# One PSUM bank for the row scores and three for the small jobs in a fused two-layer attention and expert kernel

## The chip, the core and the metric

The kernel runs on one core of one Trainium2 chip. The metric is the device time of one launch in microseconds (us). Every time below comes from this kernel's timed runs or from one profiled execution of it.

The engines are named as the profile names them. PE is TensorE (matrix multiplications; PEld is its weight load), DVE is VectorE, ACT is ScalarE, POOL is GpSimd, and SP is SyncE, which here only issues DMAs. PE writes its results into PSUM, which has eight banks of 128 partitions by 512 fp32 numbers. In this kernel DVE and ACT read them out, and POOL works only on SBUF.

## What is computed

The input is `x` with 8 batches of 256 rows and 128 features, and a context of the same shape. Four stages are added to `x` one after the other: a 16-head attention of the context, a mixture of 32 experts, a second attention, and a top-1 mixture of 8 experts. The change lies in the second attention:

```
xn, ln = layernorm(ctx), layernorm(layernorm(x))
q = ln @ Wq                                   # 16 heads of 64
k, v = [xn; ln] @ Wkv                         # 512 keys per batch
sim = (rmsnorm(q) * g_q * scale) @ (rmsnorm(k) * g_k).T
x  = x + softmax(sim) @ v @ Wout + bout
```

## The kernel before, in words

`attend_layer1` (from L1223) is the second attention. A **batch** is one of the 8. A **unit** is half of a batch's heads (8 of 16), so there are 16 units. A **step** is one pair of heads, so a unit has 4 steps and the stage has 64. Batches 1 to 6 run in a hardware loop over `b` (`flow`, L1297); the first and the last batch are written out apart.

Each step has the same parts, and each part is a word in the table `ORDER` (L1090), one string for each of the four steps of a unit:

- `rXY` (L1457, L1733): PE computes the scores of head X for 128 queries Y against all 512 keys, once and coarsely, and DVE takes their maximum into `neg_max`. This is done two steps ahead of its use. There are four in a step.
- `m` (L1448, L1627): PE transposes the four maxima of the next step, ACT copies them to `neg_rows`, and SP places them by a DMA as one more row of `q_high`.
- `sXY` (L1560, L1561, L1676 to L1681): PE computes the exact scores of head X for half Y of the keys; ACT takes the exponential twice, once rounded to fp16 and once in fp32. There are four in a step.
- `LXY` (L1738) and `P1` (L1385): the low part of the exponentials, for head 0 by DVE and for head 1 by POOL.
- `w0`, `w1` (L1473 to L1475): PE weighs the values with the probabilities of the step before; `n` (L1761, L1764): DVE divides by the sums; `a` (L1483, L1632): PE transposes the result and ACT copies it.
- `o`, `do` (L1492, L1771): once per batch, the output projection of the batch before, in fp32, and its addition to `x` by DVE.
- For the unit that follows: `k`, `q`, `v` (L1413 to L1415) are the projections of one tile of 128 rows. For `k` and `q` ACT copies the result and squares it (L1595, L1597), and `dk`, `dq` (L1703) is DVE's sum of squares. For `v` ACT copies it and `dv` (L1727) is DVE's low part. `root` (L1705 to L1721) is DVE's reciprocal square root of all the sums, 12 short instructions. `norm` (L1368, L1372) is POOL's scaling by it, `hi` (L1607) is ACT's rounding, and `low` (L1380) is POOL's low part. `tk`, `tq` (L1442, L1751) is PE's transposition of a normed tile and DVE's copy of it; SP then copies a part of it to `k_high` or `q_high` by a DMA.

Every engine walks through the same four strings and does its own share of each word, in the order of the words. So the order on each queue, and how far one engine can run ahead of another, are both set by this table. `plan_step` leaves out the words that a first or last batch does not have.

The eight PSUM banks of the stage are shared out at L1263 to L1267: `RBANKS` (2) for the row scores, `SBANKS` (3) for the exact scores, one for the weighing, and `MBANKS` (2) named `misc`. The words of `MISC` (L1137: `k q v tk tq o m a`) take the misc banks in turn, and `number` (L1168) gives each its bank and its count. PE may write a misc bank again when its last user has been read out (`emptied`, L1417). With two banks that is the word before the last one. For the row scores, PE waits at L1455 until the maximum before the last has been taken:

```
pe.wait_ge(max_done, n - RBANKS + 1)
pe.matmul(row_scores[qt % RBANKS][:], ...)
```

At the third string's first `r00`, PE also waits for the DMAs of all six transposed tiles of the next unit (L1538). At each step's first `s00` it waits for the DMA that `m` started (L1545).

Before the loop, `unit_start` (L1141) writes out the preparation of the first unit, and ends with eight row products (two steps' worth), `m`, and `root`.

Of the kernel before, what the change touches and what calls it, by code (L numbers as in the profile page):

```python
# [949 lines left out]
def prepare_layer1(nc, io, keep):  # L950
# [124 lines left out]

KQ = [("k", t) for t in range(KT)] + [("q", t) for t in range(QT)]
ROWS_AHEAD = 2
MBANKS = 2
WIDE = 2
SBANKS = 3  # L1080
RBANKS = 2


LOWS = ("V", "P")
# [3 lines left out]
ATTENDED_BY = "A"  # L1088
HALVES = 2 * PU * 2 * (KT // WIDE)
ORDER = [  # L1090
# [4 lines left out]
]  # L1095
NEWTON = 3
RSQRT_BITS = float(0x5f3759df)
# [70 lines left out]
def number(events, bank, counts):  # L1168


    counts, out, uses = list(counts), [], {}
    for event in events:
        use = uses[event[1]] if event[0] == "d" else (bank, counts[bank])
        out.append((event, use))
        if event[0] in MISC:
            uses[event] = use
            counts[bank] = counts[bank] + 1
            bank = (bank + 1) % MBANKS
    return out, bank, counts


def steps_of(first, last):
    return [plan_step(s, first, last) for s in range(2 * PU)]


def totals(events):
    return number(events, 0, (0,) * MBANKS)[2]


START_EVENTS = number(START, 0, (0,) * MBANKS)[0]  # L1190


class Batch:
# [3 lines left out]
    def __init__(self, b, first=False, last=False):  # L1197
# [4 lines left out]
        else:  # L1202
            one, whole = totals(sum(steps_of(True, False), [])), totals(sum(steps_of(False, False), []))
            self.counts = [start[i] + one[i] - whole[i] + whole[i] * b for i in range(MBANKS)]

# [17 lines left out]
def attend_layer1(nc, io, keep):  # L1223
# [3 lines left out]
    with ExitStack() as ctx:  # L1227
# [3 lines left out]
        def psum(name, shape):  # L1231
            return ctx.enter_context(nc.psum_tensor("e_" + name, shape, F32))

        def sem(name):
            return ctx.enter_context(nc.semaphore("e_" + name))
# [26 lines left out]

        row_scores = [psum(f"row_scores{i}", [P, NK1]) for i in range(RBANKS)]  # L1263

        scores = [psum(f"scores{i}", [P, WIDE, S]) for i in range(SBANKS)]
        mix = psum("mix", [P, 2, S])
        misc = [psum(f"misc{i}", [P, 512]) for i in range(MBANKS)]  # L1267
        mixed = mix[:, :, 0:QT * (D1 + 1)].rearrange("p i (t c) -> p i t c", t=QT)

        cleared, fixed = sem("cleared"), sem("fixed")  # L1270
        misc_ready, misc_taken = [sem(f"misc_ready{i}") for i in range(MBANKS)], [sem(f"misc_taken{i}") for i in range(MBANKS)]
        summed_sq, inv_steps, inv_done, normed, hi_done, low_done, v_high = (sem(n) for n in (
# [138 lines left out]
        def _(pe):  # L1411
# [38 lines left out]
            def rows(q, par, p, i, qt):  # L1450

                n = 4 * q + 2 * i + qt
                if not (isinstance(n, int) and n < RBANKS):

                    pe.wait_ge(max_done, n - RBANKS + 1)  # L1455
                h = 2 * p + i
                pe.matmul(row_scores[qt % RBANKS][:], q_high[par][0:MASK1 + 1, h, P * qt:P * qt + P], k_high[par][0:MASK1 + 1, h, :],  # L1457
                          start=True, stop=True).then_inc(rows_ready, 1)
# [232 lines left out]
        def _(dve):  # L1691
# [38 lines left out]
            def maximum(q, buf, i, qt):  # L1730
                n = 4 * q + 2 * i + qt
                dve.wait_ge(rows_ready, n + 1)
                dve.tensor_reduce(neg_max[buf][:, 2 * i + qt:2 * i + qt + 1], row_scores[qt % RBANKS][:], AX.X, ALU.max, negate=True).then_inc(max_done, 1)  # L1733

# [647 lines left out]
```

## Time and profile before

| what | us |
|---|---|
| timed runs, median of 3 (lowest, highest) | 1325.49 (1323.56, 1330.16) |
| the profiled execution's own time | 1331.85 |
| its span, first to last instruction | 1330.1 |
| the second attention, from its first projection to its last addition to `x` | about 534 to 1158 |
| DVE, PE, ACT, POOL busy over the span | 959.7, 952.3, 771.7, 591.5 |

The span and the time differ by 1.75 us, which lies around the first and the last instruction. In a timeline row the first number is the start of a group of equal instructions in us from the span's start, the second how long it lasted, and what stands in brackets at the end is the idle time of that engine before it and who ended it. Two neighbouring instructions of one engine overlap a little in the records, so the time that an instruction takes away from its engine is the distance from its start to the next start.

### The profile page before, as it was taken

To read this page: it belongs to the slowest core of one execution; us is meant where nothing else is said; L and a number is where in the kernel's file an instruction comes from. 1 tells how busy PE (TensorE), PEld (TensorE's weight loads), DVE (VectorE), ACT (ScalarE), POOL (GpSimd) and SP (SyncE) were. 2 spreads that over 40 slices of the span, in tenths; PEclk is the share of its full clock that TensorE was granted. 3 is DMA by queue.
4 is the path that set the end of the run, shared out by engine and by line. 5 is a ranking of instruction groups with operands and counts; after the bars stand their busy time and mean duration, and the time that the engine had idled before them with its cause. 6 is when DMAs were issued, how large, how long until landed. Compare 5 with 4: busy or idle time off the path is not lost. (4 is left out here: it accounts for less than half of the span.)

```text
span 1330.1 us, 28004 instructions
## 1 busy us (share of the span) xinstructions
PE 952.3 (72%) x9389; PEld 621.0 (47%) x9394; DVE 959.7 (72%) x1847; ACT 771.7 (58%) x1404; POOL 591.5 (44%) x505
## 2 busy tenths in 40 slices
PE   0378888742999921558887988888788888637655
PEld 0235555521444420125665666666565666514344
DVE  8568989767666668448888787878787887358930
ACT  1227777730555522529988897978787897441022
POOL 8010000021777730537767576767666674220324
PEclk9779999965999965759999999999899999859978
DMA  4311100010000020011111111111111111140140
GB/s 197 87 15 19 22 14 12 1 38 0 24 24 19 11 99 0 1 28 25 27 21 27 25 25 27 25 26 22 22 18 27 19 27 22 51 167 1 38 126 24
DMA packets 73839, 46.72 MB, mean 35 GB/s; under 512 B 55056, under 2 KB 70911, under 8 KB 72646
## 3 DMA queue, kind: packets, MB, share of 16 engines
q1 hardware_dynamic: 72296, 42.40, 13.3%
q0 software_dynamic: 1440, 2.82, 0.6%
q8 instruction: 80, 1.31, 0.4%
q14 instruction: 23, 0.19, 0.0%
HBM read 26.52 MB, written 8.77 MB: 27 GB/s over the span
## 5 line engine op out<-in xcount | busy, mean ns | idle before, releaser
L1385 POOL TENSOR_TENSOR e_p_lo<-e_probs,e_p_hi 128x1024 f16<-128x1024 f32 x64 | 136.3, 2129 | 127.2 <-ACT e_probs L1678 127.2
L1733 DVE TENSOR_REDUCE e_neg_max<-e_row_scores 128x1 f32<-128x512 f32 x256 | 170.1, 683 | 21.3 <-PE e_row_scores L1457 20.8
L1676 ACT ACTIVATE e_p_hi<-e_scores 128x512 f16<-128x512 f32 x256 | 153.1, 598 | 53.0 <-PE e_scores L1561 50.8
L1560 PE MATMUL e_scores<-e_q_stack,e_k_stack 128*128 128x256 f16 x512 | 127.2, 278 | 5.8 <-DVE e_p_lo L1738 5.4
L1368 POOL TENSOR_TENSOR e_raw<-e_raw,e_inv 128x512 f32<-128x512 f32 x96 | 98.9, 1043 | 70.4 <-DVE e_inv L1718 70.4
L1561 PE MATMUL e_scores<-e_q_high,e_k_high 128*128 128x256 f16 x512 | 127.3, 278 | 0.0
L1380 POOL TENSOR_TENSOR e_natural<-e_raw,e_natural 128x512 f16<-128x512 f32 x96 | 109.2, 1157 | 28.2 <-ACT e_natural L1607 27.5
L1457 PE MATMUL e_row_scores<-e_k_high,e_q_high 65*128 65x512 f16 x256 | 96.2, 395 | 33.7 <-DVE e_neg_max L1733 21.8
L716 POOL TENSOR_TENSOR c_h_lo<-c_hidden,c_h_hi 128x512 f16<-128x512 f32 x68 | 78.9, 1160 | 78.0 <-ACT c_h_hi L835 75.8
L1473 PE MATMUL e_mix<-e_v_cols,e_p_hi 128*128 128x65 f16 x1024 | 109.5, 194 | 4.4 <-POOL e_p_lo L1385 3.3
L1474 PE MATMUL e_mix<-e_v_cols,e_p_hi 128*128 128x64 f16 x1024 | 109.6, 196 | 0.0
L1475 PE MATMUL e_mix<-e_v_cols,e_p_lo 128*128 128x65 f16 x1024 | 109.1, 193 | 0.0
L1473 PEld LDWEIGHTS e_mix<-e_v_cols,e_p_hi 128*128 128x128 f16 x1024 | 96.6, 97 | 12.1 <-POOL e_p_lo L1385 4.1
L1474 PEld LDWEIGHTS e_mix<-e_v_cols,e_p_hi 128*128 128x128 f16 x1024 | 96.4, 98 | 7.9
L844 ACT ACTIVATE c_gated<-c_gate_ps 128x512 f32<-128x512 f32 x68 | 40.6, 597 | 100.3 <-PE c_gate_ps L742 100.3
L1738 DVE TENSOR_TENSOR e_p_lo<-e_scores,e_p_hi 128x512 f16<-128x512 f32 x128 | 87.6, 684 | 14.0 <-ACT e_scores L1681 12.3
L1475 PEld LDWEIGHTS e_mix<-e_v_cols,e_p_lo 128*128 128x128 f16 x1024 | 96.5, 100 | 0.0
L535 DVE TENSOR_REDUCE b_neg_max<-b_row_scores 128x2 f32<-128x512 f32 x128 | 83.2, 685 | 16.8 <-PE b_row_scores L374 15.2
L543 DVE TENSOR_TENSOR b_p_lo<-b_probs,b_p_hi 128x1024 f16<-128x1024 f32 x64 | 78.0, 1219 | 20.9 <-ACT b_p_hi L508 12.0
L505 ACT ACTIVATE b_probs<-b_scores 128x1024 f32<-128x1024 f32 x64 | 65.9, 1030 | 46.1 <-PE b_scores L394 45.4
L1442 PE MATMUL e_misc<-ident,e_natural 128*128 128x128 f16 x768 | 63.9, 232 | 37.8 <-ACT e_neg_rows L1627 18.2
L1703 DVE TENSOR_REDUCE e_sum_sq<-e_squares 128x8 f32<-128x512 f32 x96 | 65.1, 679 | 24.7 <-ACT e_squares L1597 19.7
(367 smaller groups left out, 2877.1 us busy)
## 6 DMA issues: line engine op xcount, KB each, us to landing
e_k_high<-e_k_stack SPq DMA_DIRECT2D x64, 128.0 KB, 2.7
e_q_high<-e_q_stack SPq DMA_DIRECT2D x32, 128.0 KB, 2.6
w<-in_w SPq DMA_DIRECT2D x2, 2048.0 KB, 10.1
c_w<-in_w SPq DMA_DIRECT2D x17, 192.0 KB, 2.4
placed_scratch<-in_no_rows SPq DMA_DIRECT2D x1, 2313.0 KB, 18.2
a_mask_q<-in_mask_q SPq DMA_DIRECT2D x1, 2048.0 KB, 10.2
a_mask_k<-in_mask_k SPq DMA_DIRECT2D x1, 2048.0 KB, 14.6
parts_scratch<-a_parts SPq DMA_DIRECT2D x2, 1024.0 KB, 4.0
```

Of the source, the lines that this page charges most:

```text
L1368: nc.gpsimd.tensor_tensor(raw[par][:, j], raw[par][:, j], bc(inv[:, HU * j:HU * j + HU], (P, HU, D1), 2), ALU.mult).then_inc(normed, 1)
L1380: nc.gpsimd.tensor_tensor(natural[:, j, :, at], raw[par][:, j], natural[:, j, :, hi], ALU.subtract).then_inc(low_done, 1)
L1385: nc.gpsimd.tensor_tensor(p_lo[buf][i][:], probs[i][:], p_hi[buf][i][:], ALU.subtract).then_inc(lo_done[i], 1)
L1457: pe.matmul(row_scores[qt % RBANKS][:], q_high[par][0:MASK1 + 1, h, P * qt:P * qt + P], k_high[par][0:MASK1 + 1, h, :], start=True, stop=T ...
L1473: pe.matmul(out, p_hi[buf][i][:, kt, at], values[:, 0:D1 + 1], start=first, stop=False, skip_group_check=True)
L1474: pe.matmul(out[:, 0:D1], p_hi[buf][i][:, kt, at], values[:, D1 + 1:2 * D1 + 1], start=False, stop=False, skip_group_check=True)
L1475: mm = pe.matmul(out, p_lo[buf][i][:, kt, at], values[:, 0:D1 + 1], start=False, stop=last, skip_group_check=True)
L1560: pe.matmul(out, k_stack[hf][:, h, cols], q_stack[hf][:, h, :], start=(kt % 2 == 0), stop=False, skip_group_check=True)
L1561: mm = pe.matmul(out, k_high[hf][:, h, cols], q_high[hf][:, h, :], start=False, stop=True, skip_group_check=True)
L1676: act.activation(p_hi[p % 2][i][:, at, :], scores[n % SBANKS][:], ACT.Exp).then_inc(exp_done, 1)
L1733: dve.tensor_reduce(neg_max[buf][:, 2 * i + qt:2 * i + qt + 1], row_scores[qt % RBANKS][:], AX.X, ALU.max, negate=True).then_inc(max_done, 1)
L1738: dve.tensor_tensor(p_lo[buf][i][:, at, :], scores[n % SBANKS][:], p_hi[buf][i][:, at, :], ALU.subtract).then_inc(lo_done[i], 1)
```

## The change

The constants and the table are all that is changed. The row scores get one bank instead of two, the misc words three instead of two; the total stays at eight. The words of each string are the same, in another order.

```
-MBANKS = 2
+MBANKS = 3
 WIDE = 2
 SBANKS = 3
-RBANKS = 2
+RBANKS = 1
...
 ORDER = [
-    "r00 s00 P1 norm2 w0 s01 tk0 a hi2 L00 r01 m norm3 tk1 hi3 s10 s11 low2 r10 k0 r11 L01 dk0 k1 w1 low3 n dk1",
-    "r00 norm4 hi4 P1 s00 m s01 s10 tk2 tk3 r01 norm5 L00 r10 hi5 w0 k2 L01 w1 tq0 s11 n a r11 tq1 low4 low5 dk2",
-    "L00 s00 k3 s01 o do w0 m P1 dk3 L01 s10 w1 n q0 r00 s11 r01 dq0 q1 r10 v0 r11 dq1 dv0 root a",
-    "L00 P1 w0 r00 norm0 s00 m s01 v1 dv1 s10 hi0 a r01 norm1 hi1 w1 r10 low0 s11 v2 low1 n v3 L01 dv2 dv3 r11",
+    "norm2 s00 s01 norm3 r00 hi2 m hi3 tk0 w0 P1 L00 k0 r01 dk0 s10 k1 r10 L01 w1 tk1 low2 s11 low3 r11 a dk1 n",
+    "k2 s00 m tk2 norm4 r00 norm5 hi4 s01 L00 tk3 hi5 s10 r01 a L01 w0 r10 w1 P1 n tq0 s11 tq1 low4 r11 dk2 low5",
+    "s00 o k3 a s01 P1 w0 q0 L00 s10 do r00 L01 w1 n v0 r01 dk3 m dv0 s11 r10 dq0 q1 dq1 r11 root",
+    "P1 a v1 v2 r00 norm0 m norm1 L00 w0 s00 s01 r01 dv2 hi0 hi1 s10 low0 s11 dv1 L01 w1 low1 r10 v3 n r11 dv3",
 ]
```

The wait of a row product becomes `max_done >= n`: each one waits until the maximum just before it has been taken. A misc word waits for the third before it. The bank numbers of all engines, the counts of the semaphores and `Batch`'s totals are worked out from the same two constants.

## Rows read from the trace of the kernel before

**Rows 1.** Waits on PE, 670 to 1035 us (five batches): who waited, total us, times, longest.

```profile
PE e_row_scores L1457 <- DVE e_neg_max L1733: 17.5, 13, 3.5
PE e_misc L1442 <- ACT e_neg_rows L1627: 11.6, 10, 1.3
...
PE e_misc L1483 <- ACT e_squares L1597: 7.3, 10, 0.9
```

**Rows 2.** Timeline of POOL, one unit: first `norm`, last two `low`, next unit's first `norm`.

```profile
762.17 2.04 POOL L1368 TENSOR_TENSOR e_raw<-e_raw,e_inv 128x512 f32<-128x512 f32 x2 [3.00 <-DVE e_inv L1718]
...
779.72 2.29 POOL L1380 TENSOR_TENSOR e_natural<-e_raw,e_natural 128x512 f16<-128x512 f32 x2
...
795.09 2.04 POOL L1368 TENSOR_TENSOR e_raw<-e_raw,e_inv 128x512 f32<-128x512 f32 x2 [3.02 <-DVE e_inv L1718]
```

**Rows 3.** Timeline of PE: `a`, `r11`, `tq1`, then the third string up to `r00`.

```profile
781.84 0.38 PE L1483 MATMUL e_misc<-ident,e_attended 128*128 128x128 f32 x2
782.06 0.38 PE L1457 MATMUL e_row_scores<-e_k_high,e_q_high 65*128 65x512 f16 x1
782.43 0.62 PE L1442 MATMUL e_misc<-ident,e_natural 128*128 128x128 f16 x8
782.89 0.27 PE L1560 MATMUL e_scores<-e_q_stack,e_k_stack 128*128 128x256 f16 x1
...
783.45 0.39 PE L1413 MATMUL e_misc<-wkv_hi,lat_hi 128*128 128x512 f16 x1
...
784.11 0.27 PE L1560 MATMUL e_scores<-e_q_stack,e_k_stack 128*128 128x256 f16 x1
...
784.54 0.19 PE L1473 MATMUL e_mix<-e_v_cols,e_p_hi 128*128 128x65 f16 x1
...
785.28 0.27 PE L1448 MATMUL e_misc<-ident,e_neg_max 128*4 128x128 f32 x1
...
787.21 0.38 PE L1457 MATMUL e_row_scores<-e_k_high,e_q_high 65*128 65x512 f16 x1
787.43 0.27 PE L1560 MATMUL e_scores<-e_q_stack,e_k_stack 128*128 128x256 f16 x1
```

**Rows 4.** Timeline of DVE, same unit: `n`, a maximum, `r00` with `r01`.

```profile
782.22 0.17 DVE L1761 RECIPROCAL e_inverse<-e_mix 128x4 f32<-128x4 f32 x1
...
782.76 0.68 DVE L1733 TENSOR_REDUCE e_neg_max<-e_row_scores 128x1 f32<-128x512 f32 x1
783.36 0.68 DVE L1751 COPY e_q_stack<-e_misc 128x512 f32<-128x512 f32 x1
...
788.02 1.28 DVE L1733 TENSOR_REDUCE e_neg_max<-e_row_scores 128x1 f32<-128x512 f32 x2
```

**Rows 5.** A row product that waited for its bank, on DVE and then on PE.

```profile
762.63 0.68 DVE L1733 TENSOR_REDUCE e_neg_max<-e_row_scores 128x1 f32<-128x512 f32 x1
...
763.37 0.39 PE L1457 MATMUL e_row_scores<-e_k_high,e_q_high 65*128 65x512 f16 x1 [0.69 <-DVE e_neg_max L1733]
```

**Rows 6.** ACT, same unit: first exponential of an `s`, then the next word.

```profile
783.52 0.60 ACT L1676 ACTIVATE e_p_hi<-e_scores 128x512 f16<-128x512 f32 x1
...
784.64 0.59 ACT L1595 COPY e_raw<-e_misc 128x512 f32<-128x512 f32 x1
```

**Rows 7.** DMA issues, 534 to 1160 us: name, count, KB each, median us to landing.

```profile
e_q_high<-e_q_stack SPq DMA_DIRECT2D x32, 128.0 KB, 2.6
```

**Rows 8.** The output projection on PE, and DVE's next maxima after it.

```profile
748.38 3.74 PE L1492 MATMUL e_misc<-wout,nrm 128*128 128x128 f32 x32
...
755.04 1.35 DVE L1733 TENSOR_REDUCE e_neg_max<-e_row_scores 128x1 f32<-128x512 f32 x2 [0.23 <-PE e_row_scores L1457]
```

**Rows 9.** Start of the stage: row products on PE, maxima and `root` on DVE.

```profile
578.29 1.03 PE L1457 MATMUL e_row_scores<-e_k_high,e_q_high 65*128 65x512 f16 x2 [4.23 <-DMA e_q_high<-e_q_stack]
...
578.94 2.68 DVE L1733 TENSOR_REDUCE e_neg_max<-e_row_scores 128x1 f32<-128x512 f32 x4 [4.14 <-PE e_row_scores L1457]
...
585.21 0.18 DVE L1712 TENSOR_SCALAR e_sum_sq<-e_sum_sq 128x48 f32<-128x48 f32 x1
```

**Rows 10.** PE at the loop's end: the next pass's first instruction.

```profile
802.38 0.39 PE L1457 MATMUL e_row_scores<-e_k_high,e_q_high 65*128 65x512 f16 x1 [3.75 <-issue]
```

## The prediction, made before the changed kernel was run

> **What bounds the kernel now.** I read the busy time by stage first (in the second attention no engine is full, and PE, DVE and ACT are about equally busy), then who waits for whom, then the timelines of one unit on every engine. Only those show what closes the circle.
>
> POOL gives it away. At each unit it stands idle for 3.0 us, until DVE's `root` is done, and then works without a gap until the last `low` ends at 779.72 + 2.29 = 782.01; the next unit's first `norm` starts at 795.09 [rows 2]. So the period of a unit is 795.09 - 762.17 = 32.92 us, in two legs. **Leg A**, from `root` to `tq1`: 782.43 - 762.17 = 20.26 us of POOL's work, after which PE turns the last tile [rows 2, 3]. **Leg B**, from `tq1` back to the next end of `root`: 795.09 - 782.43 = 12.66 us. PE walks from `tq1` to `r00`, 787.21 - 782.43 = 4.78 us, in which it hardly waits [rows 3]; DVE takes the first maximum 0.81 us later, at 788.02, since it is still behind, and then runs through seven words and `root` without a pause until 795.09 [rows 4, 2].
>
> PE's waits for misc banks (11.6 and 7.3 us in five batches) and for row banks (17.5 us) [rows 1] lie mostly in leg A. POOL hides them there, so long as `tq1` itself is not late.
>
> **Slots.** What a word takes from its engine, start to start. PE [rows 3]: `a` 782.06 - 781.84 = 0.22; `tq` 0.46; `k` or `q` 784.11 - 783.45 = 0.66; `s` 784.54 - 784.11 = 0.43; `w` 785.28 - 784.54 = 0.74; `r` 787.43 - 787.21 = 0.22. DVE [rows 4]: 0.60 for a maximum or any other word of 512 columns, `n` 782.76 - 782.22 = 0.54. `root` is 795.09 - 788.02 - 7 x 0.60 = 2.87, its hand-over to POOL in it. An `s` takes ACT 784.64 - 783.52 = 1.12 [rows 6].
>
> **The change, leg A.** POOL's words between `root` and `low5` are the same ones in both tables, `P1` of strings one and two among them; only their order differs. The new table puts `P1` of the second string behind `norm5`. So PE's `w1` and ACT's exponential of `s10` wait for it there (POOL needs about 4.5 us for `norm4` and `norm5` first), but both are done before `low5`. I laid out the new words with the slots above, and ACT delivers every `hi` before POOL asks for it, the closest (`hi2`) by half a microsecond. I take 0 for leg A. Bounds: below 0 nothing, since POOL is already without a gap; above, half a microsecond a unit if a `hi` comes late.
>
> **Leg B, PE's part.** From `tq1` to `r00` the new table has `tq1 r11 s00 k3 a s01 w0 q0 s10`: 0.46 + 0.22 + 0.43 + 0.66 + 0.22 + 0.43 + 0.74 + 0.66 + 0.43 = 4.25 us, against 4.78. `m` and `w1` have gone behind `r00`. The gain is 0.5 us. It is safe from the DMAs, though barely: DVE has copied `tq1` about 1.1 us after PE started it (my estimate: 0.46 for PE, 0.60 for DVE), I allow 0.3 us to the issue, and with 2.6 us to landing [rows 7] that is 4.0 us.
>
> **Leg B, DVE's part.** DVE's words before `r00` are now only `r11`, `dk2` and `L00`. It runs dry for about 1.5 us and starts `r00` 0.42 us after PE does (a product of 0.38 us [rows 3] and a hand-over). Then come `r00 L01 n r01 dk3 dv0 r10 dq0 dq1 r11 root`: 9 x 0.60 + 0.54 + 2.87 = 8.81 us, against 7.07. Three words, `L01`, `n` and `dk3`, that the old table had before `r00` now stand behind it: 1.74 us. I add 0.15 us for `dq1`, which waits for ACT. The new leg B is 4.25 + 0.42 + 8.81 + 0.15 = 13.63 us against 12.66: **+1.0 us a unit**. Bounds: 0, if DVE's dry time gets filled after all, and +1.8, if PE's half microsecond is not gained.
>
> **Units with an output projection.** `o` blocks PE for 3.7 us [rows 8]. Before, DVE's `r00` came at 755.04, and PE had started `o` at 748.38. Between `o` and `r00` the new PE order has `k3 a s01 w0 q0 s10` = 0.66 + 0.22 + 0.43 + 0.74 + 0.66 + 0.43 = 3.14 us, and before `o` one `s` and one `k` fewer but `r11` more (-0.87). So DVE's `r00` comes at 748.38 - 0.87 + 3.6 + 3.14 + 0.42 = 754.67, 0.4 us earlier, and its tail is 1.8 us longer: +1.4 us.
>
> **One row bank.** A product now waits for the maximum just before. The hand-shake is 0.42 us from product to maximum and 763.37 - 762.63 = 0.74 us from there to the next product [rows 5], 1.16 us in all. In the new table there is another word of DVE's between any two maxima, so that the two take at least 1.14 to 1.2 us anyway. Its price is zero wherever PE arrives in time. **Three misc banks** take PE's waits in leg A away, which POOL hides: zero too. If `tq1` were late for any reason, both would count at once (rivals).
>
> **Where the queues stand otherwise.** SP issues the same DMAs; `m`'s go later in the third string, but its `s00` is also later by then, 4 us or more behind. PE's 3.75 us at the loop's end [rows 10] has nothing to do with the table. The new step behind it brings `hi2` about 1.2 us sooner, but the step before it ends about that much later (its `r11` and `v3` wait for DVE): zero.
>
> **Start of the stage.** Eight products follow each other with nothing between them. At the lower clock there, the old ones took 585.21 - 578.29 = 6.92 us to `root` [rows 9]. With one bank each takes 0.65 (578.94 - 578.29) + 0.74 = 1.39 us, with `m` 11.2 us: +4.3. Three misc banks let the first transposes start earlier, which I put at -0.9. Together +3.4 us, bounds 0 and +4.3.
>
> **Sum.** Fourteen units are followed by another `root`; six of them have an `o`. 8 x 1.0 + 6 x 1.4 = 16.4, and 3.4 for the start: **+19.8 us**. The profiled execution took 1331.85 us, 6.36 above the median of the runs; against itself the sum gives 1351.7, and on the median's footing 1325.49 + 19.8 = 1345.3. Bounds of the known terms: 14 x 0 + 0 = 0, and 14 x 2.2 + 4.3 = +35.
>
> **Rivals.**
> - *The misc banks pay* (faster). If leg A is paced by PE and ACT rather than POOL, the waits for misc banks go: (11.6 + 7.3) / 5 = 3.8 us a batch [rows 1], over seven batches 26.5, less 3.4 at the start: 1302 us; with half of it, 1316. It decides at `tq1`: if PE gets there more than 0.3 us after `low5` ends in the kernel before, it is right. There it came 0.42 us after, with `r11` just before it, which leaves it a little room. For it also speaks that leg B may hold less of the tail than I think. Chance 0.22.
> - *The one row bank bites everywhere* (slower still). If PE meets an untaken maximum once a step, at the 0.69 us of the one seen [rows 5], 64 steps cost 44 us in place of the 16: about 1373 us. Against it: words stand between all maxima. Chance 0.12.
> - *Nothing moves*: DVE's dry time before `r00` is cover, so that the three moved words cost only what PE's lead gives back; with the start, 1325 to 1332 us. Chance 0.13.
> - *The change does not do what it says.* Banks, waits and counts all come from the two constants, and the sum stays at eight. Chance 0.01.
>
> PE's row product and DVE's maximum took turns over two banks without a wait in most places, and where the bank was missing the wait was 0.69 us [rows 5]. The Trainium skill (Perfetto Trace Analysis, section Optimizing Tensor Performance, Matmuls) says that independent matmul groups should rotate through different PSUM banks, so that reading one out overlaps the next. By that rule the row scores lose what the misc words gain, four products a step against at most eight misc words a step, and the sum would be that of the second rival for the one and of the first for the other; it does not say which is on the path.
>
> **How the numbers follow.** My forecast is 1345 us with a chance of 0.52. The range 1310 to 1360 takes it with nearly all its bounds, the third rival, and the nearer half of the first; it leaves out the second and the full first. A measurement of this kernel can tell about 0.5% (6.6 us) from no change. Faster by more: the first rival and a little of my own low end, 0.24. Within: 0.15. Slower: 0.61.
>
> **What would show it.** Right: POOL still works without a gap from `norm0` to `low5` in about 20 us; its idle time before the first `norm` grows from 3.0 to about 4 us; DVE is idle 1 to 2 us before the third string's `r00`; the period of a unit without `o` or loop end is near 33.9 us; PE's waits for ACT's squares and neg_rows are gone. Wrong: a period of 32 us or less, or a gap in POOL's work inside leg A, which would mean that a `hi` or `P1` has become late.

## The result, and the profile after

The changed kernel is **slower by 1.2%**: 1343.89 us (median of 4 runs, 1339.19 to 1345.48) against 1327.83 us (4 runs, 1323.56 to 1331.29) of the kernel before, a ratio of 1.0117 with a 95% interval of 1.0073 to 1.016. The forecast was 1345.0 us.

The profiled execution took 1342.71 us (span 1340.9). From the first POOL instruction of the second attention to the start of its last addition to `x` it is 1173.26 - 533.87 = 639.39 us, against 1157.54 - 534.43 = 623.11: +16.3, as the medians have it (+16.1). The two profiled executions differ by 10.9 only: what lies behind the stage took 172.5 us in the one of before and 167.7 in the one of after, and holds nothing of the change.

A **plain** unit is one without an `o`.

| from `norm0` to the next unit's `norm0`, us | before | after |
|---|---|---|
| plain unit, the steady ones | 32.90 to 32.93 | 33.16 to 33.27 |
| sum over the 14 units (8 plain, 6 with `o`) | 499.67 | 509.64 |
| of these the 8 plain ones / the 6 with `o` | 263.52 / 236.15 | 266.73 / 242.91 |
| stage start to the first unit's second `norm0` | 53.66 | 56.26 |
| last `norm0` to the last `do` | 69.78 | 73.49 |

So +9.97 in the units, +2.60 at the start, +3.71 at the end: +16.3.

The plain units ran at a granted clock of 1.00 (2.4 GHz) in both kernels, except the first, 33.02 us at 0.84 before and 34.29 at 0.78 after. The units with an `o` did not, and the table shows that this matters (the clock is TensorE's, as a mean over the unit):

| units with `o`, in order | 1 | 2 | 3 | 4 | 5 | 6 |
|---|---|---|---|---|---|---|
| longer by, us | 0.51 | 2.75 | 2.14 | 0.25 | -0.11 | 1.19 |
| clock before | 1.00 | 1.00 | 0.96 | 0.96 | 0.92 | 0.96 |
| clock after | 1.00 | 0.92 | 0.92 | 0.96 | 0.92 | 0.92 |

All but the first hold a turn of the hardware loop, at which PE stands for 3.3 to 3.9 us. Around it the granted clock is at 0.50 (1.2 GHz) for some 4 us, or for some 7, or (once, before) not at all. The unit is over 1 us longer just where the clock is lower than before. So of the 6.8 us of these six units about 3 us (6 x 0.5, by the first) belong to the change itself, an estimate. Whether the new table makes the low stretches longer, or chance does, no run separates: both lengths occur in both kernels.

PE's waits in the changed kernel, 670 to 1050 us (five batches; who waited for whom, total us, times, longest), against [rows 1]:

```profile
PE e_row_scores L1457 <- DVE e_neg_max L1733: 31.2, 51, 1.2
...
PE e_misc L1413 <- DVE e_v_cols L1727: 2.1, 10, 0.2
```

Two things are not in [rows 1] and change how it reads. In the kernel before, `m` waited for a misc bank too, and three of the 13 waits for DVE's maxima are turns of the loop, 3.5 us each, that the profile puts down to DVE:

```profile
PE e_misc L1448 <- DVE e_k_stack L1751: 4.8, 8, 0.8
```

```profile
730.34 0.39 PE L1457 MATMUL e_row_scores<-e_k_high,e_q_high 65*128 65x512 f16 x1 [3.54 <-DVE e_neg_max L1733]
```

So the waits for misc banks fell from 11.6 + 7.3 + 4.8 = 23.7 us to 2.1, and those for row banks grew from about 7 us, in 10 waits, to 31.2 in 51. Read alone, this table says that 22 us were exchanged for 24. The plain unit shows what is left of that. POOL's timeline of one, against [rows 2]:

```profile
769.31 2.04 POOL L1368 TENSOR_TENSOR e_raw<-e_raw,e_inv 128x512 f32<-128x512 f32 x2 [3.27 <-DVE e_inv L1718]
...
786.65 2.27 POOL L1380 TENSOR_TENSOR e_natural<-e_raw,e_natural 128x512 f16<-128x512 f32 x2
790.12 2.13 POOL L1385 TENSOR_TENSOR e_p_lo<-e_probs,e_p_hi 128x1024 f16<-128x1024 f32 x1 [1.20 <-ACT e_probs L1678]
797.47 2.13 POOL L1385 TENSOR_TENSOR e_p_lo<-e_probs,e_p_hi 128x1024 f16<-128x1024 f32 x1 [5.22 <-ACT e_probs L1678]
802.48 2.04 POOL L1368 TENSOR_TENSOR e_raw<-e_raw,e_inv 128x512 f32<-128x512 f32 x2 [2.88 <-DVE e_inv L1718]
```

And PE's, against [rows 3]: `tq0`, then `tq1` with nothing but `s11` ahead of it, and `r00`.

```profile
787.86 0.62 PE L1442 MATMUL e_misc<-ident,e_natural 128*128 128x128 f16 x8 [0.21 <-POOL e_natural L1380]
...
788.98 0.62 PE L1442 MATMUL e_misc<-ident,e_natural 128*128 128x128 f16 x8
...
793.22 0.38 PE L1457 MATMUL e_row_scores<-e_k_high,e_q_high 65*128 65x512 f16 x1
```

POOL works without a gap until 786.65 + 2.27 = 788.92, and `tq1` starts at 788.98. Leg A is 788.98 - 769.31 = 19.67 us, leg B 802.48 - 788.98 = 13.50. Before they were 20.26 and 12.66. Of the 0.59 us that leg A lost, 0.36 are at its end, where `tq1` started 0.42 us behind POOL's last `low` and now starts 0.06 behind it. The other 0.23 are in POOL's own part, 19.84 us before and 19.61 after, mostly a short wait of the kernel before, behind its `norm0` and `norm1`:

```profile
764.39 2.27 POOL L1380 TENSOR_TENSOR e_natural<-e_raw,e_natural 128x512 f16<-128x512 f32 x2 [0.18 <-ACT e_natural L1607]
```

DVE's timeline of the same unit, against [rows 4], from its `L00` to the start of `root`:

```profile
791.54 0.69 DVE L1738 TENSOR_TENSOR e_p_lo<-e_scores,e_p_hi 128x512 f16<-128x512 f32 x1
793.63 0.69 DVE L1733 TENSOR_REDUCE e_neg_max<-e_row_scores 128x1 f32<-128x512 f32 x1 [1.40 <-PE e_row_scores L1457]
...
797.77 1.30 DVE L1703 TENSOR_REDUCE e_sum_sq<-e_squares 128x8 f32<-128x512 f32 x2
799.00 0.68 DVE L1733 TENSOR_REDUCE e_neg_max<-e_row_scores 128x1 f32<-128x512 f32 x1
799.59 0.18 DVE L1712 TENSOR_SCALAR e_sum_sq<-e_sum_sq 128x48 f32<-128x48 f32 x1
```

DVE runs dry for 1.40 us, takes `r00` 0.41 us after PE starts it, and then needs 802.48 - 793.63 = 8.85 us until POOL can start behind `root`. Hold on to one more pair of numbers, which I passed over at first: POOL's `P1` ends at 797.47 + 2.13 = 799.60, and `root` begins at 799.59.

At the start of the stage each row product waits for the maximum before it. PE's timeline and the start of DVE's `root`, against [rows 9]:

```profile
575.96 0.61 PE L1457 MATMUL e_row_scores<-e_k_high,e_q_high 65*128 65x512 f16 x1 [4.56 <-DMA e_q_high<-e_q_stack]
577.35 0.61 PE L1457 MATMUL e_row_scores<-e_k_high,e_q_high 65*128 65x512 f16 x1 [0.79 <-DVE e_neg_max L1733]
...
587.25 0.18 DVE L1712 TENSOR_SCALAR e_sum_sq<-e_sum_sq 128x48 f32<-128x48 f32 x1
```

Product to product it is 1.39 us, the number of the prediction, and from the first product to `root` 587.25 - 575.96 = 11.29 us (forecast 11.2, before 6.92).

### The profile page after: what moved, and what is told of

The parts are those of the page before. It is cut to its first block and busy times, and to the rows that moved or that the text cites. A ratio compares the mean times of both kernels' runs of the same rounds, so it can differ in the third digit from the quotient of the medians.

```text
span 1340.9 us, 27886 instructions
## 1 busy us (share of the span) xinstructions
PE 964.1 (72%) x9394; PEld 626.7 (47%) x9394; DVE 957.7 (71%) x1847; ACT 770.0 (57%) x1404; POOL 594.0 (44%) x505
## 5 line engine op out<-in xcount | busy, mean ns | idle before, releaser
L1733 DVE TENSOR_REDUCE e_neg_max<-e_row_scores 128x1 f32<-128x512 f32 x256 | 175.1, 684 | 72.5 <-PE e_row_scores L1457 72.1
L1457 PE MATMUL e_row_scores<-e_k_high,e_q_high 65*128 65x512 f16 x256 | 102.9, 402 | 56.5 <-DVE e_neg_max L1733 51.4
L1738 DVE TENSOR_TENSOR e_p_lo<-e_scores,e_p_hi 128x512 f16<-128x512 f32 x128 | 87.4, 683 | 11.3 <-ACT e_scores L1681 10.9
L543 DVE TENSOR_TENSOR b_p_lo<-b_probs,b_p_hi 128x1024 f16<-128x1024 f32 x64 | 78.0, 1219 | 20.9 <-ACT b_p_hi L508 11.9
L1703 DVE TENSOR_REDUCE e_sum_sq<-e_squares 128x8 f32<-128x512 f32 x96 | 64.5, 680 | 25.8 <-ACT e_squares L1597 20.9
L877 DVE TENSOR_TENSOR c_upped<-c_up_ps,c_gated 128x512 f32<-128x512 f32 x68 | 47.0, 692 | 49.5 <-PE c_up_ps L742 48.3
```

What stands on the lines that cost most here:

```text
L1738: dve.tensor_tensor(p_lo[buf][i][:, at, :], scores[n % SBANKS][:], p_hi[buf][i][:, at, :], ALU.subtract).then_inc(lo_done[i], 1)
```

## The experiments

All times are medians. A ratio is to the kernel before on the same chip, with its 95% interval. The "circle" below is the dependence of one unit on the last: `root`, leg A, `tq1`, leg B, `root`.

**First question: is one row bank free, and is the third misc bank worth nothing, as I had said of both?** Two runs keep the old table and change the banks alone.

Run 1:

```
-MBANKS = 2
+MBANKS = 3
-RBANKS = 2
+RBANKS = 1
 ORDER = (the old table)
```

> The table of before with the banks of after (one for the row scores, three misc). Theory (the unit is two legs, and one bank costs 0.56 us wherever two maxima are neighbours on DVE in the leg from tq1 to root): the old table has r00 r01 and r10 r11 side by side there, so a plain unit takes 32.92 + 1.1 = 34.0 us, 14 units 15.6 us, the start 2.6 and the last batch about 3.5: about 1349 us. Rival (the third misc bank pays 3.8 us a batch): 1310 to 1325 us, with plain units at 32.5 or less.

Measured: 1402.76 us, ratio 1.0519 (1.0474 to 1.0564), 68.5 us over the kernel before. A plain unit takes 37.7 to 39.0 us. The expectation of about 1349 was far off.

Run 2 also leaves the misc words two banks, so that seven are used:

```
 MBANKS = 2
-RBANKS = 2
+RBANKS = 1
 ORDER = (the old table)
```

> The table of before with one row-score bank and still two misc banks (seven PSUM banks used). Theory (POOL hides PE's waits for misc banks): like e1 except for the start, 1.0 us more there, so 1350 us, and plain units within 0.1 us of e1's. Rival (the third bank pays): 15 to 26 us above e1.

Measured: 1436.18 us, ratio 1.0767 (1.0724 to 1.081), a plain unit mostly 41.0. So with one row bank and the old table the third misc bank is worth 1436.18 - 1402.76 = 33 us, where I had said 0 to 1.

The trace of run 1 shows where one bank hurts. PE, in the fourth string and behind it:

```profile
787.39 0.44 PE L1457 MATMUL e_row_scores<-e_k_high,e_q_high 65*128 65x512 f16 x1 [2.38 <-DVE e_neg_max L1733]
...
794.08 0.39 PE L1457 MATMUL e_row_scores<-e_k_high,e_q_high 65*128 65x512 f16 x1 [1.78 <-DVE e_neg_max L1733]
```

ACT, which then lacks scores:

```profile
790.46 0.60 ACT L1676 ACTIVATE e_p_hi<-e_scores 128x512 f16<-128x512 f32 x1 [1.57 <-PE e_scores L1561]
```

And POOL, whose `low` waits for ACT's `hi` in the middle of leg A:

```profile
786.19 2.04 POOL L1368 TENSOR_TENSOR e_raw<-e_raw,e_inv 128x512 f32<-128x512 f32 x2 [4.10 <-DVE e_inv L1718]
...
799.53 1.16 POOL L1380 TENSOR_TENSOR e_natural<-e_raw,e_natural 128x512 f16<-128x512 f32 x1 [3.78 <-ACT e_natural L1607]
```

PE does not lose the 0.74 us of a hand-shake, it loses its **lead**. With two banks PE may draw one row product while DVE is still in `root`, and go on to `s` behind it. With one it stands at the second `r` until DVE has come out of `root` and taken the first, and every `s` queued behind that `r` is late for ACT. The wait at 787.39 is over just after `root`.

Behind that wait PE is slow as well. From 787.39 to 791.0 us the granted clock is 0.50 to 0.57, where it had been 1.00 until then, and an `s` matmul takes 0.42 us in place of 0.27:

```profile
789.36 0.42 PE L1560 MATMUL e_scores<-e_q_stack,e_k_stack 128*128 128x256 f16 x1
```

The plain units of run 1 fall into two groups, 37.7 to 37.9 us at a mean clock of 0.95 and 38.8 to 39.0 at 0.91. Those of run 2 ran at 0.88 and those of the kernel before at 1.00. So a part of the 68.5 us, of the order of 1 us for each such stretch (an estimate from the two groups), goes with the clock, and the rest is the lead. Run 5 below has the lead's part alone.

**Second question: what in the new table makes one bank bearable?** Two runs on the changed kernel put parts of the old order back.

Run 3 puts the whole third string back:

```
-    "s00 o k3 a s01 P1 w0 q0 L00 s10 do r00 L01 w1 n v0 r01 dk3 m dv0 s11 r10 dq0 q1 dq1 r11 root",
+    "L00 s00 k3 s01 o do w0 m P1 dk3 L01 s10 w1 n q0 r00 s11 r01 dq0 q1 r10 v0 r11 dq1 dv0 root a",
```

> The changed kernel with only its third string put back to the old one. Theory: leg A stays at 19.7 us; leg B is the old one with two hand-shakes of 0.56 and r11 behind tq1, 12.66 + 1.1 + 0.2 = 14.0, so a plain unit takes 33.7 us against 33.2 and the kernel 1343.9 + 14 x 0.5 = 1350 us. If instead the new third string is what costs (the three words behind r00), putting it back returns 0.3 us a unit or more: 1340 us or less.

Measured: 1378.4 us, ratio 1.0333 (1.0294 to 1.0372), a plain unit 35.0 to 36.6, most of the excess in leg A (20.9 to 22.6). With `v0` and `dv0` near the end of the string, a `v` of the fourth string waits for its bank on PE:

```profile
773.03 0.39 PE L1413 MATMUL e_misc<-wkv_hi,ctx_hi 128*128 128x512 f16 x1 [1.63 <-DVE e_v_cols L1727]
```

and everything queued behind it comes late, so that POOL's first `low` waits for `hi0`:

```profile
775.69 2.04 POOL L1368 TENSOR_TENSOR e_raw<-e_raw,e_inv 128x512 f32<-128x512 f32 x2 [4.09 <-DVE e_inv L1718]
780.57 2.27 POOL L1380 TENSOR_TENSOR e_natural<-e_raw,e_natural 128x512 f16<-128x512 f32 x2 [2.84 <-ACT e_natural L1607]
```

Run 5 moves one word, so that the row product stands ahead of the scores:

```
-    "P1 a v1 v2 r00 norm0 m norm1 L00 w0 s00 s01 r01 dv2 hi0 hi1 s10 low0 s11 dv1 L01 w1 low1 r10 v3 n r11 dv3",
+    "P1 a v1 v2 r00 norm0 m norm1 L00 w0 r01 s00 s01 dv2 hi0 hi1 s10 low0 s11 dv1 L01 w1 low1 r10 v3 n r11 dv3",
```

> The changed kernel with one word moved: in the fourth string r01 goes ahead of s00 and s01. Theory (with one bank PE can't run past a product until DVE has taken the maximum before it, so what matters is what stands behind such a product on PE): r00's maximum is behind root, so PE waits at r01 until about 0.7 us after root, s00 and s01 start 2.3 us later than now, hi0 with them, and POOL gets a gap of about 2 us behind norm1. Plain units 35.2 us against 33.2, the kernel about 1343.9 + 14 x 2.1 = 1373 us. Rival (one bank costs only the hand-shake of neighbouring maxima): L00 still stands between the two maxima, so less than 0.2 us a unit, 1346 us or less.

Measured: 1381.35 us, ratio 1.0345 (1.032 to 1.0369), a plain unit 35.55 against the 35.2 expected. PE stands at `r01` behind `root`:

```profile
782.57 0.39 PE L1457 MATMUL e_row_scores<-e_k_high,e_q_high 65*128 65x512 f16 x1 [2.10 <-DVE e_neg_max L1733]
```

and POOL again has a gap before the first `low`:

```profile
786.36 2.27 POOL L1380 TENSOR_TENSOR e_natural<-e_raw,e_natural 128x512 f16<-128x512 f32 x2 [2.33 <-ACT e_natural L1607]
```

In the changed kernel `s00 s01` lie between `r00` and `r01` of the fourth string, which gives PE and ACT work while DVE is in `root`. Moving that one word costs 2.4 us a unit, and PE's granted clock is 1.00 in the steady ones, as in the changed kernel: this is lost lead and nothing else. What one bank costs depends on the table, not on the bank count alone.

**Third question: what sets leg B?** Run 4 takes DVE's `dk3` out of the row of words behind `r00`, into DVE's dry time:

```
-    "... s10 do r00 L01 w1 n v0 r01 dk3 m dv0 s11 r10 dq0 q1 dq1 r11 root",
+    "... s10 do dk3 r00 L01 w1 n v0 r01 m dv0 s11 r10 dq0 q1 dq1 r11 root",
```

> The changed kernel with one word moved: DVE does dk3 before r00, in its dry 1.4 us. Theory as predicted (leg B is the sum of DVE's words behind r00): 0.6 us less a unit, 8.4 us in all, about 1335.5 us. Rival (DVE's dq1 waits for ACT's squares of q1, which ended at 798.36 just as dq1 started): dq1 stays where it is and at most 0.15 us a unit are won, about 1342 us.

Measured: 1345.93 us, ratio 1.0088 (1.0057 to 1.0118). The plain unit is 33.17 to 33.18 us, unchanged: the 0.6 us taken from DVE came back as waits for ACT. DVE:

```profile
796.91 0.69 DVE L1727 TENSOR_TENSOR e_v_cols<-e_misc,e_v_cols 128x512 f16<-128x512 f32 x1 [0.30 <-ACT e_v_cols L1615]
...
798.12 1.50 DVE L1703 TENSOR_REDUCE e_sum_sq<-e_squares 128x8 f32<-128x512 f32 x2
```

`dv0` waits 0.30 us, and `dq0` and `dq1` together take 1.50 in place of 1.30, since the second has to wait. DVE's words are not the only thing that ends at `root`.

Run 6 therefore also brings `q1` forward, past `s11`, so that ACT has its squares earlier:

```
-    "... r01 m dv0 s11 r10 dq0 q1 dq1 r11 root",
+    "... r01 m dq0 q1 s11 dv0 r10 dq1 r11 root",
```

> e4 and in addition q1 (and dq0) ahead of s11 in the third string, so that ACT squares q1 about 1 us earlier. Theory (dk3's move gave nothing because dq1 waited for ACT): now DVE's words close up and root ends 0.6 us earlier; plain units 32.6 us against 33.2, 8.4 us in all, about 1335.5 us. Rival (leg B is set by something else, PE's r10 and r11): plain units stay within 0.15 us of 33.2.

Measured: 1356.64 us, ratio 1.0172 (1.0155 to 1.0189), a plain unit 33.98 to 34.4 where 32.6 was expected. DVE did not wait for ACT behind `r00` any more, and `root` began 806.38 - 796.39 = 9.99 us after `tq1`, 0.62 earlier than in the changed kernel (799.59 - 788.98). But `root` took longer. DVE:

```profile
806.38 1.62 DVE L1712 TENSOR_SCALAR e_sum_sq<-e_sum_sq 128x48 f32<-128x48 f32 x1
808.04 0.19 DVE L1713 TENSOR_SCALAR e_halved<-e_sum_sq 128x48 int32<-128x48 int32 x1
```

and POOL at the same time:

```profile
805.83 2.12 POOL L1385 TENSOR_TENSOR e_p_lo<-e_probs,e_p_hi 128x1024 f16<-128x1024 f32 x1 [6.17 <-ACT e_probs L1678]
810.72 2.04 POOL L1368 TENSOR_TENSOR e_raw<-e_raw,e_inv 128x512 f32<-128x512 f32 x2 [2.76 <-DVE e_inv L1718]
```

`root`'s first instruction has 48 numbers a partition, takes 0.18 us elsewhere, and here 1.62: it ended when `P1` did (805.83 + 2.12 = 807.95). It waits for nothing of `P1` in the program. It was so in all 14 units (1.42 to 1.69), while the stage's first two, beside no `P1`, took 0.18 and 0.19. With `s11` later, ACT's exponential and so `P1` came later, and held `root`.

Runs 7 and 8 had tried to shorten leg B in the kernel before, with the same idea of DVE's words alone. Run 7 puts `dv0` behind `root` (and `v1 dv1` of the fourth string behind `s10`):

```
-    "... r01 dq0 q1 r10 v0 r11 dq1 dv0 root a",
-    "L00 P1 w0 r00 norm0 s00 m s01 v1 dv1 s10 hi0 a r01 ...",
+    "... r01 dq0 q1 r10 v0 r11 dq1 root dv0 a",
+    "L00 P1 w0 r00 norm0 s00 m s01 s10 v1 dv1 hi0 a r01 ...",
```

> The kernel before (two row banks, two misc banks) with dv0 moved behind root in the third string, and v1 and dv1 behind s10 in the fourth, since v1 needs the bank that dv0 empties. Theory (the period is POOL's leg A plus DVE's words up to root): root comes one word, 0.6 us, earlier; plain units 32.3 us against 32.92, 8.4 us in all, 1327.8 - 8.4 = 1319.4 us. Rival (PE or ACT has no slack left and sets the period): plain units within 0.15 us of 32.9, no change.

Measured: 1361.12 us, ratio 1.0213 (1.018 to 1.0246), a plain unit mostly 35.4. Leg B fell by only 0.27 us, to 12.39, since `P1` held `root` here too, in all 14 units (0.30 to 0.39 us in place of 0.18). Leg A grew to 23.0 us. The next `m` needs the misc bank that `dv0` empties, and stands there through all of `root`, with `s01` behind it (`root`'s first instruction on DVE, then `m` on PE):

```profile
767.53 0.31 DVE L1712 TENSOR_SCALAR e_sum_sq<-e_sum_sq 128x48 f32<-128x48 f32 x1
...
771.15 0.27 PE L1448 MATMUL e_misc<-ident,e_neg_max 128*4 128x128 f32 x1 [2.69 <-DVE e_v_cols L1727]
```

Run 8 puts `r11` and `dv0` behind `root`, `s11` later in the third string, and `m` behind `s10` in the fourth:

```
-    "... q0 r00 s11 r01 dq0 q1 r10 v0 r11 dq1 dv0 root a",
-    "L00 P1 w0 r00 norm0 s00 m s01 v1 dv1 s10 hi0 a r01 norm1 hi1 w1 ...",
+    "... q0 r00 q1 r01 dq0 s11 r10 v0 dq1 root r11 dv0 a",
+    "L00 P1 w0 r00 norm0 s00 s01 s10 m v1 dv1 hi0 a r01 norm1 hi1 w1 ...",
```

> As e7, and r11 behind root too, with q1 ahead of s11 and, in the fourth string, m behind s10 (m needs r11's maximum). Theory: root comes 1.2 us earlier; plain units 31.7 us, 1327.8 - 16.8 = 1311 us, if leg A keeps POOL without a gap. Against it: PE waits at m until 1.3 us behind root, so v1 and a come later and a hi may be late; then the gain is eaten up and the time is 1320 us or more.

Measured: 1382.31 us, ratio 1.0371 (1.0349 to 1.0393), a plain unit 36.1 to 37.4. Here both happen: leg A has gaps (it takes 22.8 to 24.0 us), and `root` is held by `P1` again, on DVE

```profile
774.14 1.68 DVE L1712 TENSOR_SCALAR e_sum_sq<-e_sum_sq 128x48 f32<-128x48 f32 x1
```

beside, on POOL, a `P1` that ends at 773.65 + 2.13 = 775.78:

```profile
773.65 2.13 POOL L1385 TENSOR_TENSOR e_p_lo<-e_probs,e_p_hi 128x1024 f16<-128x1024 f32 x1 [8.90 <-ACT e_probs L1678]
```

Both forecasts (1319 and 1311) fell.

**Fourth question: does POOL's `P1` really hold `root`?** Run 9 is run 6 with the fourth string's `P1` behind `norm1`, so that POOL is idle while `root` runs:

```
-    "P1 a v1 v2 r00 norm0 m norm1 L00 w0 ...",
+    "a v1 v2 r00 norm0 m norm1 P1 L00 w0 ...",
```

> The run with q1 ahead of s11, whose root took 4.18 us in place of 2.73 in every plain unit: its first instruction began at 806.38 and lasted 1.62 us in place of 0.18, until POOL's P1 (805.83 + 2.12 = 807.95) was over. Here the fourth string's P1 stands behind norm1, so POOL is idle while root runs. If DVE's first root instruction was held up by POOL's P1, it is back at 0.18 us and root at 2.73, leg B is 1.4 us shorter than in that run, leg A 2.1 us longer (P1's work now lies in it), a plain unit 34.7, the whole 1364 us. Rival, root is long for a reason of its own (q1's squares or the semaphore): it stays at 4.2 us with POOL idle, a plain unit is 36.1, the whole 1385 us.

Measured: 1369.99 us, ratio 1.0328 (1.0272 to 1.0383), a plain unit 34.6 to 35.8. DVE's first instruction of `root` is back at 0.18 us (0.19 once), in all 16 of the stage:

```profile
806.16 0.18 DVE L1712 TENSOR_SCALAR e_sum_sq<-e_sum_sq 128x48 f32<-128x48 f32 x1
```

POOL idle throughout, and `P1` behind the norms:

```profile
809.04 2.04 POOL L1368 TENSOR_TENSOR e_raw<-e_raw,e_inv 128x512 f32<-128x512 f32 x2 [9.59 <-DVE e_inv L1718]
811.04 2.12 POOL L1385 TENSOR_TENSOR e_p_lo<-e_probs,e_p_hi 128x1024 f16<-128x1024 f32 x1
```

So the hold-up is shown, with one word moved. The move itself costs more than it frees, since the 2.1 us of `P1` and what waits for it (PE's `w`, 2.08 us once) now lie in leg A. A plain unit took the expected 34.6 us where the granted clock was 1.00, and 35.8 where it was 0.90. The Trainium skill (SBUF — State Buffer, section Who interferes with whom) says that DVE and GpSimd share one pair of SBUF ports as an exclusive lock that is held for a whole instruction, and that DVE's `tensor_scalar` can ask for it. The traces here agree: the instruction ends about 0.05 us behind `P1`. They also show which of DVE's words this does not touch: in the fourteen profiles over 3,700 of its words of 512 columns ran wholly or almost wholly beside a POOL instruction, and every one took 0.67 to 0.70 us. Each of those reads PSUM, or, as `dk` and `dq` do, is a `tensor_reduce` of one SBUF operand. `root`'s first instruction is a `tensor_scalar` from SBUF to SBUF, and no other instruction of `root` ever ran beside POOL.

**Fifth question: is there a better version?** Three runs on the changed kernel. Runs 10 and 11 have `s11` earlier, so that `P1` is over in time.

Run 10 takes two words from DVE and brings `q1` forward:

```
-    "... s10 do r00 L01 w1 n v0 r01 dk3 m dv0 s11 r10 dq0 q1 dq1 r11 root",
-    "P1 a v1 v2 r00 norm0 m norm1 L00 w0 s00 s01 r01 dv2 hi0 hi1 s10 ...",
+    "... s10 do dk3 r00 L01 w1 n s11 r01 q1 m v0 dq0 r10 dq1 r11 root dv0",
+    "P1 a v1 r00 norm0 m norm1 L00 w0 s00 s01 r01 hi0 v2 hi1 dv2 s10 ...",
```

> The changed kernel with dk3 ahead of r00, s11 and q1 earlier in the third string, dv0 behind root, and v2 later in the fourth. DVE then has two words fewer between r00 and root and ACT's squares of q1 come before dq1. Worked out with the slots: s11 starts at 794.0 in place of 795.2, P1 ends near 798.4 in place of 799.6, root starts at 798.4: leg B 1.2 us shorter. Theory (leg B is set by DVE's words behind r00, with P1's end as its floor): a plain unit 32.0 to 32.2, root's first instruction still near 0.18 us, leg A unchanged at 19.7, the whole about 1328 us. Rival (the misc words behind dv0 wait in the fourth string, as in the run on the kernel before with dv0 behind root): leg A 21 us or more with a gap in POOL's work, the whole 1350 us or more.

Measured: 1398.66 us, ratio 1.0537 (1.0493 to 1.0582), a plain unit 37.2. The rival was right, and worse than I gave it: `m` waits for `dv0`'s bank on PE through all of `root`,

```profile
821.97 0.37 PE L1448 MATMUL e_misc<-ident,e_neg_max 128*4 128x128 f32 x1 [2.94 <-DVE e_v_cols L1727]
```

and POOL for `hi0`:

```profile
821.39 2.04 POOL L1368 TENSOR_TENSOR e_raw<-e_raw,e_inv 128x512 f32<-128x512 f32 x2 [2.90 <-DVE e_inv L1718]
827.47 2.28 POOL L1380 TENSOR_TENSOR e_natural<-e_raw,e_natural 128x512 f16<-128x512 f32 x2 [4.04 <-ACT e_natural L1607]
```

Run 11 leaves `dv0` ahead of `root`, and the fourth string as it is:

```
+    "... s10 do dk3 r00 L01 w1 n s11 r01 q1 m v0 dq0 r10 dq1 dv0 r11 root",
```

> The changed kernel with dk3 ahead of r00 and s11 and q1 earlier in the third string, dv0 still ahead of root, the fourth string as in the changed kernel. Against the run with dk3 alone ahead of r00 the wait of dq1 for ACT goes. Theory: root starts 0.6 us earlier, P1 is over by then, a plain unit 32.6, the whole about 1336 us. Rival (root is bound to s11 and P1 whatever DVE does): the unit stays at 33.17, 1344 us.

Measured: 1338.99 us, ratio 1.0096 (1.0064 to 1.0129), a plain unit 33.23 to 33.26: nearly the rival's 33.17, while the whole lies between the theory's 1336 and the rival's 1344. `P1` is over 0.6 us before `root` (796.24 + 2.13 = 798.37), and what is left is ACT. DVE:

```profile
797.18 0.69 DVE L1703 TENSOR_REDUCE e_sum_sq<-e_squares 128x8 f32<-128x512 f32 x1 [0.42 <-ACT e_squares L1597]
...
798.98 0.18 DVE L1712 TENSOR_SCALAR e_sum_sq<-e_sum_sq 128x48 f32<-128x48 f32 x1
```

ACT's squares of `q1` started at 796.45, behind nine half-microsecond instructions in a row from 792 on without a pause.

Run 12 draws `q1` ahead of `s10`:

```
+    "s00 o k3 a s01 P1 w0 q0 L00 q1 do dk3 r00 L01 w1 n s10 s11 r01 m v0 dq0 dq1 r10 dv0 r11 root",
```

> The changed kernel with q1 drawn ahead of s10 in the third string, s10 and s11 behind w1 and dk3 ahead of r00, dv0 ahead of root as before. In the last run dq1 still waited 0.52 us for ACT's squares of q1 (DVE idle before 797.18), and P1 was over 0.66 us ahead of root. Theory, three things end at root (DVE's words behind r00, ACT's squares of q1, POOL's P1): dq1 no longer waits, PE's r00 comes 0.23 us later, root 0.3 to 0.4 us earlier, its first instruction at 0.18 to 0.3 us, a plain unit 32.8 to 32.9, the whole 1333 us: nearly the kernel before, and not under it. Rival, ACT is not among them (the wait of dq1 moves on to another word): the unit stays at 33.2 and the whole at 1339 us.

Measured: 1346.72 us, ratio 1.0116 (1.009 to 1.0143), a plain unit 33.68 to 33.70, not 32.8. `dq1` no longer waits, but `q1` pushed `s11` back on ACT by its two instructions, so `P1` came at 798.24 (ending at 800.37) and held `root` by 0.33 us. ACT was late for another word besides, since `dv0` now waited 0.23 us for it, and leg A was 0.2 us longer:

```profile
799.91 0.51 DVE L1712 TENSOR_SCALAR e_sum_sq<-e_sum_sq 128x48 f32<-128x48 f32 x1
```

**What follows.** At `root` three chains end within some tenths of a microsecond: DVE's words behind `r00`, ACT's squares of `q1` (runs 4 and 11), and ACT's exponential of `s11` with POOL's `P1` behind it (runs 6 and 12). The last two share one engine that runs without a pause, so whichever is put first, the other is late. No version tried beats the kernel before, so the question of a better one stays open. Run 11 has the lowest median of those on three misc banks, but its interval overlaps that of the changed kernel.

## Why the prediction was right, and where it was not

The forecast of 1345.0 us is 1.1 us from the median, and slower was the likeliest case. That it is so near is luck. The change was forecast at +19.8 us and measured at +16.1; 2.3 us of the nearness come from the baseline, whose median was 1325.49 in the forecast's three runs and 1327.83 in four. And within the sum errors cancel. What was right is the mechanism of leg B and of the start.

- **Leg B, +1.0 a unit: right in kind, a little too large.** PE from `tq1` to `r00` took 793.22 - 788.98 = 4.24 us (forecast 4.25), the hand-over 0.41 (0.42), DVE's dry time 1.40 (1.5), from `r00` to the end of `root` 8.85 (8.81 + 0.15). The sum is 13.50 against 13.63, so +0.84. But it is more than DVE's words: the runs showed that ACT and `P1` end within some tenths of a microsecond, so taking a word from DVE gives nothing back (run 4).
- **Leg A, "I take 0", "below 0 nothing": mis-sized.** It fell by 0.59 us, to 19.67. POOL was not "already without a gap": 0.18 us of the gain is its wait for ACT's `hi0` in the kernel before. The larger part, 0.36, is at the end of the leg. Before, `tq1` came 0.42 us after `low5` ended, since `a` and `r11` stood ahead of it on PE; now 0.06 us. I had that 0.42 in hand (it is the test of the first rival, which it passed) and counted it to the wrong side: PE's place in front of `tq1` was part of the circle. The rival was right about that and wrong about the price, 3.8 us a batch. A plain unit is thus 0.25 us longer, not 1.0.
- **Units with `o`, +1.4:** leg B grew by 1.10 us in each, and leg A fell by 0.59 in the one without a turn of the loop: +0.51 there. The others vary from -0.11 to +2.75 with the granted clock around the turn, for which the prediction had no term (it put PE's idle time there at "zero"). The eight plain ones gave +3.2 us in all (1.27 of it in the first, the one at the lower clock), the six others +6.8: 10.0 in place of 16.4.
- **Start, +3.4: right.** Row products took 4.37 us more (forecast 4.3), and the first one came 1.77 us earlier (42.09 us from the stage's start against 43.86; forecast 0.9), which leaves +2.6. Not all of the 1.77 is the third misc bank: in the three other profiles with two of them (runs 2, 7, 8) the first product came at 42.77 to 43.01, and in all ten with three at 42.02 to 42.09. The bank's share is 0.7 to 1.0.
- **End of the stage: left out, +3.7 us.** The last batch has no `norm` and `low` behind which the rest hides; POOL's seven `P1` there waited 29.4 us for ACT in place of 26.2. The banks alone make this end 12.9 us longer (82.71 us in run 1, with the old table), so one row bank is dear there and the new order takes most of it back. Its granted clock was 0.95 before and 0.91 after, but run 12 took 71.7 us at 0.98, so the clock isn't all of the 3.7. How the rest splits over the words wasn't tested. With this term missing, and 6.4 us too much in the units and 0.8 at the start, the sum of +19.8 came near +16.3.
- **One row bank, "its price is zero wherever PE arrives in time":** no run contradicts it for the new table, but none shows it either: two row banks beside three misc banks would need nine. For it speaks that in the plain unit DVE works from `r00` to `root` without a pause, 8.85 us for words of 8.81. But the reason was wrong. I looked for two maxima next to each other on DVE. What counts is what PE has queued behind an `r` that must wait through `root`: up to 68.5 us with the old table (run 1, the low clock and the last batch in it), and 32 with one word moved (run 5 stands 48.0 us over the kernel before, the changed kernel 16.1). The second rival had the right kind of mechanism for another table.
- **Three misc banks, "zero too": wrong as a general statement.** In the changed kernel it can't be tested, since the new table on two misc banks would wait in a circle (`m` for the bank of `v1`, whose `dv1` stands behind `r01`). Beside one row bank and the old table the third was worth 33 us (run 2 against run 1). The first rival, that they pay on balance, is out: PE's waits for misc banks went, and a unit got longer.
- **POOL's idle time before `norm`** did not grow to 4 us; it is 2.88 to 3.28. What grew was PE's and ACT's part of leg B, in which POOL waits before `P1`.
- **Waits on PE.** The prediction took all of the 17.5 us in [rows 1] for waits for row banks. About 10.5 of them are turns of the loop, so that these waits went from 7 to 31.2 us and not from 17.5.
- **Cited rule.** The Trainium skill's rule (Perfetto Trace Analysis, section Optimizing Tensor Performance, Matmuls) is that independent matmul groups should rotate through different PSUM banks, so that reading one out overlaps the next. The waits agree: with one bank more, PE waited 21.6 us less for misc banks, and with one less, 24 us more for the row bank. Neither number is in the time of a plain unit.
- **Upper bound.** The sum takes 2.2 us a unit, where the bounds of the two legs, 1.8 and 0.5, add up to 2.3. That would be +36.5 in place of +35 and changes nothing.

## What to carry to other kernels

A PSUM bank in a kernel whose engines walk through one fixed order is worth what the engine in front can do behind it, not the hand-shake: before giving one away, find the longest thing that the reading engine does between two reads (here `root`) and see what the writing engine has queued behind its next write. Where the writing engine is PE, look at the granted clock behind the wait as well: in run 1 it was at 0.50 to 0.57 for the 3.6 us that followed 2.4 us of standing still, in run 5 it stayed at 1.00 after 2.1. Before shortening a chain, look for what else ends at the same point, and also for an instruction on POOL that is just over when DVE's begins; here `P1` ended within 0.13 us of the start of `root` in the plain units of both kernels (0.4 us ahead of it in the changed kernel's units with an `o`), and every attempt to start `root` earlier ran into it, into ACT, or into the bank that `dv0` empties. Split the period of a loop at the instruction that two engines hand over, and forecast the first and the last pass apart.

## What the hardware showed that was not expected

- A DVE `tensor_scalar` of 128x48 fp32 in SBUF, 0.18 us alone, took up to 1.94 us beside a POOL `tensor_tensor` of 128x1024, and ended 0.04 to 0.05 us behind it (runs 6, 7, 8 and 12). Nothing in the program orders the two. The profile books the time as DVE busy, with no wait and no releaser, so it is to be seen by the duration of the row alone.
- Its mark is on POOL too: where `P1` held `root`, POOL was idle for 2.75 or 2.76 us from the end of `P1` to `norm0`, to a hundredth the same in runs 6, 7, 8 and 12; in the kernel before it was 2.97 to 3.02.
- PE's granted clock is not the same from one unit to the next with the same instructions. In run 1 plain units took 37.7 to 37.9 us at 0.95 and 38.8 to 39.0 at 0.91, in run 9 34.6 at 1.00 and 35.8 at 0.90. Two kernels are better compared by units at the same clock.
